# Windowed attention and routed experts: values projected once a token and spread by DMA, turns of normalised tokens a step later

## The chip, the core and the metric

The kernel runs on one core of one Trainium2 chip. TensorE multiplies matrices into PSUM, VectorE and ScalarE read PSUM and SBUF, GpSimd works on SBUF, and SyncE mostly issues DMAs. The metric is the time on the device in microseconds (us) from launch to end. The profile is of one execution; its span goes from the first to the last instruction, and a little of the time lies outside it.

## The reference, cut to what matters

```python
Q = (x @ Wq.T).reshape(B, S, HKV, G, HEAD_DIM)     # B, S = 2, 2048; 4 groups of 4 heads, 8 wide
K = (x @ Wk.T).reshape(B, S, HKV, HEAD_DIM)
V = (x @ Wv.T).reshape(B, S, HKV, HEAD_DIM)
# scores of each token against the 257 tokens around it, softmax, weighted sum of V_win
out = jnp.einsum('bskgw,bswkd->bskgd', attn, V_win).reshape(B, S, HQ * HEAD_DIM) @ Wo.T
x = _layernorm(x + out)
# router: softmax of x @ Wr over 8 experts, the best two, their weights
# expert: (silu(x @ gate) * (x @ up)) @ down, 128 -> 256 -> 128; weighted sum of two
x = _layernorm(x + experts)
```

All of it is float32, and the width of a token is 128.

## The kernel before

The 4096 tokens are 32 tiles of 128 (16 tiles for each of the two sequences) and 8 groups of 512. The attention runs as a loop of steps `s`, written out for each engine by a function `step(s)`; the order of the instructions is fixed by hand, and semaphores carry the dependencies. In step `s` the engines work on several tiles at once:

- TensorE makes the scores of tile `s+2` with queries as rows (`scores_a`, "A items", L736 to L751), from which VectorE takes the largest score (`largest_score`, L1368, L1372, and `negated`, L1381). `maxima(s+1)` (L817) turns the negated maxima of tile `s+1`, ScalarE copies them to `stage` (L1103), and four small DMAs of SyncE (L511) write them as extra rows of `q`.
- TensorE makes the scores of tile `s` again with keys as rows (`scores_b`, "B items", L766 to L787), the maxima included, and ScalarE takes their exponentials (L1095). The three pairs of PSUM banks `pX` go round between A and B items.
- `values(s, 0)` and `values(s-1, n)` (L811) multiply the exponentials by the values `vx`; `sums`, `output` and VectorE finish tile `s-1` (L824, L830, L1416 to L1441).
- Every fourth step (`ln_group`, steps 5, 9, 13, ...) GpSimd runs `norm(m)` for four finished tiles: twelve tiny operations on 128x4 and four of 128x128 (L646), the last of which let the tile be used (`x1_done`).
- `turn(t)` (L835) transposes the normalised tile `t` into `pM`, in the same bank and with the same semaphore step as `maxima(s+1)`; ScalarE copies both out. `x_tile(s)` says which tile: `s - 6`. Four turned tiles are multiplied by the router's weights in `logits` (L840, steps 10, 14, ...).
- The projections of group `n` stand in single steps (`projected(s)`): queries at `4n-7`, keys at `4n-5`, values at `4n-4`; for group 1 at steps -4, -3 and -1. They use one PSUM bank, `pM`, in the order of the dictionary `SMALL`, whose numbers are what the semaphores `m_psum` and `m_evac` count.

The values stand out. `vx` needs a key of 64 tokens on 128 partitions, each half of 32 tokens twice (once for each of two heads of a pair), with a mask of blocks. Before, the host gave `xT` with each 32 tokens written twice, so a group of `xt` has 1024 columns, and `values_of` (L862) makes eight matmuls of 128 of these columns by `wv_sb` (32 wide):

```python
            def values_of(bank, n):
                for c in range(8):
                    mm = pe.matmul(bank[:, c * 32:(c + 1) * 32], xt[:, n % 2, c * P:(c + 1) * P], wv_sb[:],
```

ScalarE copies the 256 columns to `vs`, and GpSimd's `spread_values(n)` (L593) multiplies them by the mask into `vx`, in the step of the projection. In float32 a matmul is two records of the trace.

After the attention the experts run as 44 halves in units `k`, two blocks of 128 rows each (L975 to L1016); the last steps of the attention's tail (`s` from 32, turns and logits among them) are put into the first units by `MOE_STEPS`.

SyncE's queue is in order too: in step `s` first the four rows of maxima, then the writes (`queries_out`) or reads (`queries_in`) of the queries' scratch in HBM, the next `xt`, and other loads.

Of the kernel before, what the change touches and what calls it, by code (L numbers as in the profile page):

```python
# [115 lines left out]
FIRST = -4  # L116
# [68 lines left out]
def x_tile(s):  # L185

    t = s - 6
    return t if 0 <= t < NT else None
# [36 lines left out]
def projected(s):  # L225

    for n in range(1, NGR):
        first = FIRST if n == 1 else 4 * n - 7
        for what, at in (("q", first), ("k", first + (1 if n == 1 else 2)), ("v", first + 3)):
            if s == at:  # L230
                return n, what
    return None
# [26 lines left out]
def attention_moe(nc, x, xT, wq, wk, wv, wo, wr, wgu, wd, consts, out, q_scr, xs, ys):  # L259
    with ExitStack() as ctx:  # L260
# [16 lines left out]
        xt = sb("xt", [P, 2, 2 * GT])  # L277
        vs = sb("vs", [P, 8, 32])
# [79 lines left out]
        v_done = sem("v_done")  # L358
        q_out = sem("q_out")
# [103 lines left out]
        def _(sp):  # L463
            xg = xT.rearrange("d (n t) -> d n t", t=2 * GT)
            sp.dma_start(xt[:, 0, :], xg[:, 0, :]).then_inc(xt_in, 16)
# [5 lines left out]
            sp.dma_start(xt[:, 1, :], xg[:, 1, :]).then_inc(xt_in, 16)  # L471
# [9 lines left out]
            def queries_in(n):  # L481
                sp.wait_ge(q_out, 128 * (n + 1))
                if n >= 2:
                    sp.wait_ge(b_psum, b_done(4 * (n - 2) + 3))
                for j in range(3):
                    read_queries(sp, n, j)

# [16 lines left out]
            def step(s):  # L504
# [9 lines left out]
                for n in range(1, NGR):  # L514
                    if s == (FIRST + 1 if n == 1 else 4 * n - 6):
                        queries_out(n)
                    if s == 4 * n - 4:
                        queries_in(n)
                    if s == 4 * n - 4 and n + 1 < NGR:
                        sp.wait_ge(m_evac, SMALL["v", n])  # L520
                        sp.wait_ge(xt_in, 16 * (n + 1))
                        sp.dma_start(xt[:, (n + 1) % 2, :], xg[:, n + 1, :]).then_inc(xt_in, 16)
# [20 lines left out]
            read_first_queries(sp, 2, 1, 4, q_in)  # L543
            for s in range(FIRST, NT):
                step(s)
# [31 lines left out]
        def _(pool):  # L577
# [10 lines left out]
            def spread_values(n):  # L588
                if n >= 4:
                    t = min(4 * (n - 4) + 4, TPS - 1)  # L590
                    pool.wait_ge(pv_done, ROUND_AT[t, len(rounds(t)) - 1])
# [6 lines left out]
            def project(n, what):  # L598
# [20 lines left out]
                if what == "v":  # L619
                    pool.wait_ge(m_evac, SMALL["v", n])  # L620
                    spread_values(n)
# [4 lines left out]
            pool.wait_ge(v0_copied, 1)  # L626
            pool.wait_ge(s_zero, 2)
            spread_values(0)
# [51 lines left out]
            def step(s):  # L680
                if projected(s) is not None:
                    project(*projected(s))
# [27 lines left out]
        def _(pe):  # L710
# [146 lines left out]
            def tokens(n):  # L857
                return xt[:, n % 2, :].rearrange("p (c o k) -> p c o k", o=2, k=32)[:, :, 0, :]

            def values_of(bank, n):  # L860
                for c in range(8):
                    mm = pe.matmul(bank[:, c * 32:(c + 1) * 32], xt[:, n % 2, c * P:(c + 1) * P], wv_sb[:],  # L862
                                   start=c == 0, stop=True, skip_group_check=True)
# [177 lines left out]
        def _(act):  # L1041
# [10 lines left out]
            act.activation(vs[:].rearrange("p c e -> p (c e)"), pX[1][:, 0, 0:256], ACT.Copy).then_inc(v0_copied, 1)  # L1052
# [15 lines left out]
            def project(n, what):  # L1068
# [7 lines left out]
                else:  # L1076
                    act.wait_ge(v_done, n)
                    act.activation(vs[:].rearrange("p c e -> p (c e)"), pM[:, 0:256], ACT.Copy).then_inc(m_evac, 1)
# [124 lines left out]
        def _(dve):  # L1203
# [253 lines left out]
            dve.tensor_copy(ks[:], pM[:]).then_inc(m_evac, 1)  # L1457

# [155 lines left out]
```

## Time and profile before

| what | value |
|---|---|
| median of 3 runs | 549.03 us |
| lowest and highest of them | 544.09 and 549.33 us |
| time of the profiled execution | 550.67 us |
| its span | 548.8 us |
| TensorE busy in it | 483.2 us (88%) |
| VectorE, ScalarE, GpSimd busy | 363.0, 294.6, 241.8 us |
| mean granted TensorE clock | 0.895 |

The profiled execution is 1.6 us above the median, and 1.9 us of it lie outside the span. The granted clock is a share of 2.4 GHz; it has two levels in this trace, 1.0 and 0.5 (1.2 GHz). The attention ends at about 375 us of the span, the experts' matmuls at about 517 us.

### The profile page before, as it was taken

To read this page: it belongs to the slowest core of one execution; us is meant where nothing else is said; L and a number is where in the kernel's file an instruction comes from. 1 tells how busy PE (TensorE), PEld (TensorE's weight loads), DVE (VectorE), ACT (ScalarE), POOL (GpSimd) and SP (SyncE) were. 2 spreads that over 40 slices of the span, in tenths; PEclk is the share of its full clock that TensorE was granted. 3 is DMA by queue.
4 is the path that set the end of the run, shared out by engine and by line. 5 is a ranking of instruction groups with operands and counts; after the bars stand their busy time and mean duration, and the time that the engine had idled before them with its cause. 6 is when DMAs were issued, how large, how long until landed. Compare 5 with 4: busy or idle time off the path is not lost.

```text
span 548.8 us, 11862 instructions
## 1 busy us (share of the span) xinstructions
PE 483.2 (88%) x3865; PEld 292.4 (53%) x3865; DVE 363.0 (66%) x823; ACT 294.6 (54%) x512; POOL 241.8 (44%) x329
## 2 busy tenths in 40 slices
PE   5699999999998999999999999987999999999700
PEld 2354454454453545344544554434788888888600
DVE  1556867867865446667767888755347765767785
ACT  2125655656655433446556666664565555655551
POOL 2501155455334030223284487600870727776772
PEclk9558999999999555779999999989999999999955
DMA  6633333342235215212621513102242555553462
GB/s 169 99 51 67 80 59 98 79 71 86 42 54 140 39 40 88 68 30 51 127 38 24 98 36 93 41 28 62 76 130 81 164 156 144 146 136 96 107 167 59
DMA packets 84156, 46.92 MB, mean 85 GB/s; under 512 B 40608, under 2 KB 79520, under 8 KB 83424
## 3 DMA queue, kind: packets, MB, share of 16 engines
q1 hardware_dynamic: 65360, 31.04, 25.7%
q0 software_dynamic: 4096, 8.40, 5.7%
q10 hardware_dynamic: 14640, 6.73, 4.4%
q8 instruction: 33, 0.54, 0.5%
q14 instruction: 27, 0.22, 0.1%
HBM read 26.47 MB, written 19.40 MB: 84 GB/s over the span
## 4 chain that ended last, share of the span: by engine, by line
PE 72%; DVE 8%; ACT 6%; POOL 5%; issue 5%; DMA 3%; ACTq 0%; SPq 0%; POOLq 0%; DVEq 0%
PE pV L811 15%; PE pX L736 6%; PE pX L775 6%; PE pX L1016 6%; ACT probs L1095 4%; PE pV L824 4%; PE pX L996 3%; PE pX L998 3%; PE pX L997 3%; PE pX L748 3%; PE pM L862 3%; PE pV L1007 3%; PE pX L787 2%; PE pM L830 2%; PE pX L766 2%
## 5 line engine op out<-in xcount | busy, mean ns | idle before, releaser
L1095 ACT ACTIVATE probs<-pX 128x1024 f32<-128x1024 f32 x152 | 152.9, 1024 | 73.4 <-PE pX L766 58.4
L1368 DVE TENSOR_REDUCE mp<-pX 128x4 f32<-128x1024 f32 (+4 forms) x128 | 150.7, 1185 | 41.0 <-PE pX L740 31.2
L811 PE MATMUL pV<-probs,vx 128*32 128x512 f32 (+1 forms) x736 | 96.1, 589 | 2.4 <-DVE attT L1419 2.0
L676 POOL DMA_INDIRECT probs<-ys,source x64 | 64.5, 1008 | 30.6 <-issue 25.7
L664 POOL DMA_INDIRECT xs<-xr,slot x64 | 63.0, 985 | 31.4 <-issue 17.6
L736 PE MATMUL pX<-kx,q 48*128 48x512 f32 (+4 forms) x256 | 63.3, 494 | 4.2 <-DMA q<-q_scr 4.0
L775 PE MATMUL pX<-q,kx 50*128 50x512 f32 x248 | 64.9, 520 | 0.5 <-DVE mp L1368 0.4
L1471 DVE TENSOR_TENSOR probs<-probs,pX 128x512 f32<-128x512 f32 x44 | 30.2, 686 | 34.4 <-ACT probs L1157 34.4
L1016 PE MATMUL pX<-we,probs 128*128 x352 | 47.0, 276 | 1.1 <-ACT vx L1169 1.1
L1016 PEld LDWEIGHTS pX<-we,probs 128*128 128x128 f32 x352 | 42.7, 192 | 2.0 <-issue 1.9
L1416 DVE RECIPROCAL rden<-pV 128x128 f32<-128x128 f32 x32 | 30.4, 951 | 18.8 <-PE pV L824 18.8
L1157 ACT ACTIVATE probs<-pX 128x512 f32<-128x512 f32 x44 | 26.3, 597 | 30.2 <-PE pX L998 29.2
L775 PEld LDWEIGHTS pX<-q,kx 50*128 50x128 f32 x248 | 25.9, 205 | 26.5 <-issue 17.1
L603 POOL CAST kh<-ks 128x512 fp32r<-128x512 f32 x7 | 4.3, 610 | 78.0 <-ACT ks L1072 78.0
L996 PE MATMUL pX<-we,qh 128*128 x88 | 38.6, 438 | 0.0
L1434 DVE TENSOR_TENSOR xr<-pM,xr 128x128 f32<-128x128 f32 x32 | 9.3, 292 | 39.4 <-PE pM L830 38.9
L736 PEld LDWEIGHTS pX<-kx,q 48*128 48x128 f32 x256 | 27.0, 209 | 14.7 <-POOL kt L605 5.6
L616 POOL CAST qh<-qs 128x512 fp32r<-128x512 f32 x7 | 4.3, 609 | 69.1 <-ACT qs L1075 68.5
L998 PE MATMUL pX<-we,ql 128*128 x88 | 34.7, 394 | 0.0
L997 PE MATMUL pX<-we,qh 128*128 x88 | 34.5, 392 | 0.0
L766 PE MATMUL pX<-mask 64*128 64x256 bf16 (+1 forms) x184 | 31.5, 338 | 0.0
L748 PE MATMUL pX<-kx,q 48*128 48x64 f32 x240 | 21.5, 303 | 9.0 <-ACT probs L1095 8.8
(151 smaller groups left out, 829.1 us busy)
## 6 DMA issues: line engine op xcount, KB each, us to landing
xt<-xs SPq DMA_DIRECT2D x88, 64.0 KB, 1.9
ys<-vx ACTq DMA_DIRECT2D x44, 128.0 KB, 2.1
q<-q_scr SPq DMA_DIRECT2D x42, 128.0 KB
xt<-xT SPq DMA_DIRECT2D x8, 512.0 KB, 5.7
q_scr<-qh SPq DMA_DIRECT2D x32, 64.0 KB, 2.3
q<-stage SPq DMA_DIRECT2D x128, 2.0 KB
xr<-x SPq DMA_DIRECT2D x8, 256.0 KB, 6.0
raw<-wgu SPq DMA_DIRECT2D x4, 512.0 KB, 5.9
```

Of the source, the lines that this page charges most:

```text
L664: pool.indirect_dma_start(xs[ph][:, :], bass.IndirectOffsetOnAxis(ap=slot[:, t, k:k + 1], axis=0), tile(t), None, bounds_check=ROWS - 1, o ...
L676: pool.indirect_dma_start(yin[:, t % YIN, k, :], None, ys[ph][:, :], bass.IndirectOffsetOnAxis(ap=source[:, t, k:k + 1], axis=0), bounds_c ...
L736: mm = pe.matmul(bank[:, pr, 0:64 * (k1 - k0)], q_cols(t, KA, pr, i, i + 1), k_cols(KA, pr, k0, k1), start=True, stop=True, skip_group_che ...
L766: return pe.matmul(bank[:, pr, a * P:b * P].rearrange("p (c g t) -> p c g t", g=G, t=32), mask_rows(pr, M_ONEK, M_ONEK + P), mask_rows(pr, ...
L775: mm = pe.matmul(bank[:, pr, :], k_cols(KB, pr, k0, k0 + 2), q_cols(t, KB, pr, 0, 4), start=True, stop=True, skip_group_check=True)
L811: mm = pe.matmul(pV[row:row + 32, cols], vx[:, chunk, pr, :], src[:, pr, cols], start=n == 0, stop=True, skip_group_check=True)
L996: pe.matmul(to, xh[:, k % 2, rows], hi, start=True, stop=False, skip_group_check=True)
L997: pe.matmul(to, xh[:, k % 2, rows], lo, start=False, stop=False, skip_group_check=True)
L998: mm = pe.matmul(to, xl[:, k % 2, rows], hi, start=False, stop=True, skip_group_check=True)
L1016: mm = pe.matmul(pX[2][:, 1, h * D:(h + 1) * D], hidT[:, k % 2, at:at + P], we[:].bitcast(F32)[:, bass.ds(expert[k, h] + 4 * F + f * D, D) ...
L1095: act.activation(dst, src[:], ACT.Exp).then_inc(exp_done, 1)
L1368: dve.tensor_reduce(mp[:, t % 2, 0, :, i, :], src[:, :, 0:2 * n].rearrange("p r (c v k) -> p r v c k", v=NV, k=32), AX.XY, ALU.max).then_i ...
```

## The change

Turns: `x_tile(s)` becomes `s - 7`, so each `turn(t)` comes one step later. `logits` stays in its step, which now is that of the group's last turn.

Values: `xT` holds each token once, `xt` uses 512 columns a group, and `values_of` makes four matmuls. Their 128 columns go to a new tile `vd` (token on partition), from there by one DMA to a scratch `v_scr` in HBM, and by four DMAs back into `vs` with each 32 tokens on two groups of 32 partitions. SyncE issues both: the write in the step of the projection (`values_out`), the reads a step later (`values_in`). GpSimd's spread comes two steps after the projection. The first two groups are special: group 1's values are projected at step -3, evicted by VectorE, and both groups' reads and spreads stand at steps -2 and -1.

```diff
-FIRST = -4
+FIRST = -5
...
-    t = s - 6
+    t = s - 7
...
-        for what, at in (("q", first), ("k", first + (1 if n == 1 else 2)), ("v", first + 3)):
+        for what, at in (("q", first), ("k", first + (1 if n == 1 else 2)), ("v", first + (2 if n == 1 else 3))):
...
-            sp.dma_start(xt[:, 0, :], xg[:, 0, :]).then_inc(xt_in, 16)
+            xg = xT.rearrange("d (n t) -> d n t", t=GT)
+            sp.dma_start(xt[:, 0, 0:GT], xg[:, 0, :]).then_inc(xt_in, 16)
...
+            def values_out(n):
+
+                wait(sp, v_in[n % 2], 64 * (n // 2))
+                sp.dma_start(v_scr[n % 2].rearrange("(c p) e -> p c e", p=P), vd[:, n % 2]).then_inc(v_out[n % 2], 16)
+
+            def values_in(n):
+
+                sp.wait_ge(v_out[n % 2], 16 * (n // 2 + 1))
+                wait(sp, v_done, n)
+                for a in range(2):
+                    for o in range(2):
+                        row = 64 * a + 32 * o
+                        sp.dma_start(vs[row:row + 32, :, :], v_scr[n % 2].rearrange("(c a k) e -> a k c e", a=2, k=32)[a]
+                                     ).then_inc(v_in[n % 2], 16)
...
+                for n in range(NGR):
+                    if s == (n - 2 if n < 2 else STEP_OF["v", n] + 1):
+                        values_in(n)
+                    if n and s == STEP_OF["v", n]:
+                        sp.wait_ge(m_evac, SMALL["v", n])
+                        values_out(n)
...
             def spread_values(n):
+                pool.wait_ge(v_in[n % 2], 64 * (n // 2 + 1))
...
-                if what == "v":
-                    pool.wait_ge(m_evac, SMALL["v", n])
-                    spread_values(n)
...
             def step(s):
+                for n in range(NGR):
+                    if s == (n - 2 if n < 2 else STEP_OF["v", n] + 2):
+                        spread_values(n)
...
-                return xt[:, n % 2, :].rearrange("p (c o k) -> p c o k", o=2, k=32)[:, :, 0, :]
+                return xt[:, n % 2, 0:GT]
...
-                for c in range(8):
+                for c in range(4):
...
-                    act.wait_ge(v_done, n)
-                    act.activation(vs[:].rearrange("p c e -> p (c e)"), pM[:, 0:256], ACT.Copy).then_inc(m_evac, 1)
+                    wait(act, v_out[n % 2], 16 * (n // 2))
+                    act.activation(vd[:, n % 2].rearrange("p c e -> p (c e)"), pM[:, 0:P], ACT.Copy).then_inc(m_evac, 1)
...
+            dve.wait_ge(m_psum, SMALL["v", 1])
+            dve.tensor_copy(vd[:, 1].rearrange("p c e -> p (c e)"), pM[:, 0:P]).then_inc(m_evac, 1)
```

Three places show how the rows move. First TensorE in step 6, the first with a turn before the change; `nmz` are the negated maxima, `xr` the normalised tile, and the names in brackets are the semaphores waited for. Before:

```order
L811 MATMUL pV<-probs,vx 32x512 [waits exp_done]
L811 MATMUL pV<-probs,vx 32x512 x3
L817 MATMUL pM<-identr,nmz 128x128 [waits nm_done,m_evac,z_done]
L835 MATMUL pM<-cst,xr 128x128 [waits x1_done]
L736 MATMUL pX<-kx,q 128x512 [waits exp_done]
```

and after, at the same place:

```order
L836 MATMUL pV<-probs,vx 32x512 [waits exp_done]
L836 MATMUL pV<-probs,vx 32x512 x3
L842 MATMUL pM<-identr,nmz 128x128 [waits nm_done,m_evac,z_done]
L761 MATMUL pX<-kx,q 128x512 [waits exp_done]
L761 MATMUL pX<-kx,q 128x512
```

The wait for `x1_done` has left this step; the same turn now stands behind the maxima of the next one.

Second TensorE's start, from the values of group 0 to the first A item; the bank `pM` holds the projections of group 1. Before:

```order
L862 MATMUL pX<-wv_sb,xt 128x32 x7
L871 MATMUL pM<-xt,wq_sb 128x512 [waits xt_in]
L869 MATMUL pM<-xt,wk_sb 128x512 [waits xt_in,m_evac]
L736 MATMUL pX<-kx,q 128x256 [waits s_const,q_first,v0_copied,k_ops,q_split]
...
L740 MATMUL pX<-mask 128x64 x2
L862 MATMUL pM<-wv_sb,xt 128x32 [waits xt_in,m_evac]
L862 MATMUL pM<-wv_sb,xt 128x32 x7
L736 MATMUL pX<-kx,q 128x512 [waits a_max]
```

and after:

```order
L887 MATMUL pX<-wv_sb,xt 128x32 x3
L896 MATMUL pM<-xt,wq_sb 128x512 [waits xt_in]
L894 MATMUL pM<-xt,wk_sb 128x512 [waits xt_in,m_evac]
L887 MATMUL pM<-wv_sb,xt 128x32 [waits xt_in,m_evac]
L887 MATMUL pM<-wv_sb,xt 128x32 x3
L761 MATMUL pX<-kx,q 128x256 [waits s_const,q_first,v0_copied,k_ops,q_split]
```

Group 1's values moved from between two A items to the place ahead of the first, and are four matmuls and not eight.

Third SyncE's queue at the start, from the first reads of queries to the rows of maxima of tile 0 (`q<-stage`). Before:

```order
L447 DMA q<-q_scr 16x1536 x4
L433 DMA q_scr<-qh 512x1x32 [waits q_split]
L433 DMA q_scr<-qh 512x1x32 x3
L433 DMA q_scr<-ql 512x1x32 [waits q_split]
L433 DMA q_scr<-ql 512x1x32 x3
L511 DMA q<-stage 1x4x128 [waits m_evac]
```

and after:

```order
L450 DMA q<-q_scr 16x1536 x4
L494 DMA v_scr<-vd 128x4x32 [waits v0_copied]
L436 DMA q_scr<-qh 512x1x32 [waits q_split]
L436 DMA q_scr<-qh 512x1x32 x3
L436 DMA q_scr<-ql 512x1x32 [waits q_split]
L436 DMA q_scr<-ql 512x1x32 x3
L494 DMA v_scr<-vd 128x4x32 [waits m_evac]
L503 DMA vs<-v_scr 32x8x32 [waits v_out0]
L503 DMA vs<-v_scr 32x8x32 x3
L529 DMA q<-stage 1x4x128 [waits m_evac]
L529 DMA q<-stage 1x4x128 x3
L503 DMA vs<-v_scr 32x8x32 [waits v_done,v_out1]
```

Six DMAs now stand between the reads of queries and the maxima of tile 0, and four more behind these.

## Rows read from the trace of the kernel before

**Rows 1.** The page: granted clock in 40 slices, shares of the chain.

```profile
PEclk9558999999999555779999999989999999999955
...
PE 72%; DVE 8%; ACT 6%; POOL 5%; issue 5%; DMA 3%; ACTq 0%; SPq 0%; POOLq 0%; DVEq 0%
```

**Rows 2.** The chain that ended last: start us, us, engine, tile, line, count.

```profile
26.24 3.55 PE pM L862 x16
...
74.79 1.90 PE pM L862 x16
...
210.54 3.55 PE pM L862 x16
```

**Rows 3.** What TensorE waited for: us in total, times, longest.

```profile
PE pX L748 <- ACT probs L1095: 8.8, 22, 0.5
...
PE pM L835 <- POOL xr L646: 3.0, 4, 1.9
...
PE pM L849 <- issue: 0.7, 1, 0.7
```

**Rows 4.** The timeline around 175 us, ScalarE and TensorE; idle before in brackets.

```profile
170.04 0.60 ACT L1075 ACTIVATE qs<-pM 128x512 f32<-128x512 f32 x1 [0.86 <-PE pM L871]
...
176.98 0.30 PE L835 MATMUL pM<-cst,xr 128*128 128x128 f32 x1 [1.90 <-POOL xr L646]
```

**Rows 5.** Windows: length, busy PE, PEld, DVE, ACT, POOL, then clock, DMA share, GB/s.

```profile
177.00:178.00 1.00, 1.00 (x7) 0.47 (x11) 0.24 (x1) 0.41 (x2) 1.00 (x2) 0.69 0.06 16
...
178.00:224.00 46.00, 45.92 (x259) 22.94 (x252) 23.80 (x48) 15.95 (x24) 6.88 (x8) 0.50 0.30 58
225.00:232.00 7.00, 5.86 (x65) 3.29 (x67) 5.24 (x8) 4.70 (x9) 2.63 (x6) 0.99 0.26 77
...
225.00:226.00 1.00, 1.00 (x10) 0.73 (x10) 0.22 (x2) 0.43 (x3) 0.00 (x0) 0.92 0.00 0
...
232.00:239.00 7.00, 7.00 (x34) 2.51 (x26) 4.11 (x16) 2.05 (x2) 4.73 (x12) 0.51 0.01 2
...
371.00:379.00 8.00, 5.98 (x59) 3.18 (x52) 3.54 (x13) 2.05 (x6) 0.00 (x0) 1.00 0.25 68
```

**Rows 6.** The chain: values and an A item at either clock.

```profile
143.17 0.43 PE pX L736 x2
...
151.28 1.00 PE pV L811 x8
...
185.74 1.86 PE pV L811 x8
...
189.50 0.72 PE pX L736
```

**Rows 7.** VectorE's timeline around the first values among A items.

```profile
30.64 1.23 DVE L1368 TENSOR_REDUCE mp<-pX 128x4 f32<-128x1024 f32 x1 [2.67 <-PE pX L740]
```

**Rows 8.** The start: a piece of the chain, and a window.

```profile
1.19 4.68 DMA wq_sb<-wq
...
4.00:8.00 4.00, 1.99 (x3) 0.99 (x4) 0.00 (x0) 0.00 (x0) 0.00 (x0) 1.00 0.95 287
```

**Rows 9.** SyncE's and TensorE's timeline at the start, and the scratch's DMAs.

```profile
21.25 2.64 SPq L433 DMA_DIRECT2D q_scr<-ql  x4
25.10 10.93 SPq L511 DMA_DIRECT2D q<-stage  x8
...
33.90 0.77 PE L775 MATMUL pX<-q,kx 50*128 50x512 f32 x2
...
L511 SPq DMA_DIRECT2D q<-stage x12: 572/573/727, 25.1 to 46.8; - x12
...
DMA to landing us min/median/max: 1.9/2.3/3.4
```

**Rows 10.** TensorE's timeline in a unit with turns and logits.

```profile
390.02 1.06 PE L840 MATMUL pM<-wr_sb,x1T 128*128 128x8 f32 x8 [0.35 <-ACT x1T L1107]
391.40 0.30 PE L835 MATMUL pM<-cst,xr 128*128 128x128 f32 x1 [0.32 <-issue]
```

More of the change, by code:

```diff
@@ L256, in k_ready, with attention_moe @@
     return 5 * n + 4
-def attention_moe(nc, x, xT, wq, wk, wv, wo, wr, wgu, wd, consts, out, q_scr, xs, ys):
+def attention_moe(nc, x, xT, wq, wk, wv, wo, wr, wgu, wd, consts, out, q_scr, v_scr, xs, ys):
     with ExitStack() as ctx:
@@ L277, in attention_moe @@
         xt = sb("xt", [P, 2, 2 * GT])
+        vd = sb("vd", [P, 2, 4, 32])
         vs = sb("vs", [P, 8, 32])
@@ L358, in attention_moe @@
         v_done = sem("v_done")
+        v_out = [sem(f"v_out{i}") for i in range(2)]
+        v_in = [sem(f"v_in{i}") for i in range(2)]
         q_out = sem("q_out")
@@ L463, in _ @@
         def _(sp):
-            xg = xT.rearrange("d (n t) -> d n t", t=2 * GT)
-            sp.dma_start(xt[:, 0, :], xg[:, 0, :]).then_inc(xt_in, 16)
+            xg = xT.rearrange("d (n t) -> d n t", t=GT)
+            sp.dma_start(xt[:, 0, 0:GT], xg[:, 0, :]).then_inc(xt_in, 16)
             sp.dma_start(wq_sb[:], wq).then_inc(s_wq, 16)
@@ L470, in _ @@
             sp.wait_ge(xt_in, 16)
-            sp.dma_start(xt[:, 1, :], xg[:, 1, :]).then_inc(xt_in, 16)
+            sp.dma_start(xt[:, 1, 0:GT], xg[:, 1, :]).then_inc(xt_in, 16)
             def queries_out(n):
@@ L521, in step @@
                         sp.wait_ge(xt_in, 16 * (n + 1))
-                        sp.dma_start(xt[:, (n + 1) % 2, :], xg[:, n + 1, :]).then_inc(xt_in, 16)
+                        sp.dma_start(xt[:, (n + 1) % 2, 0:GT], xg[:, n + 1, :]).then_inc(xt_in, 16)
+                for n in range(NGR):
[4 more added lines that the diff above has]
+                        values_out(n)
                 if s % 4 == 0 and 0 <= s < NT:
@@ L543, in _ @@
             read_first_queries(sp, 2, 1, 4, q_in)
+            sp.wait_ge(v0_copied, 1)
+            values_out(0)
             for s in range(FIRST, NT):
@@ L625, in _ @@
             spread_keys(0, 1).then_inc(k_ops, 1)
-            pool.wait_ge(v0_copied, 1)
             pool.wait_ge(s_zero, 2)
-            spread_values(0)
             def norm(m):
@@ L1051, in _ @@
             act.wait_ge(p0_psum, 3)
-            act.activation(vs[:].rearrange("p c e -> p (c e)"), pX[1][:, 0, 0:256], ACT.Copy).then_inc(v0_copied, 1)
+            act.activation(vd[:, 0].rearrange("p c e -> p (c e)"), pX[1][:, 0, 0:P], ACT.Copy).then_inc(v0_copied, 1)
             act.wait_ge(k_ops, 2)
@@ L1590 @@
         "x": x,
-        "xT": np.ascontiguousarray(np.broadcast_to(
-            x.T.reshape(D, TOK // 32, 1, 32), (D, TOK // 32, 2, 32)).reshape(D, 2 * TOK)),
+        "xT": np.ascontiguousarray(x.T),
         "wq": np.ascontiguousarray(
@@ L1608 @@
     q_scr = nc.dram_tensor("q_scr", (2, 2, NR, 16, GT // 32, G, 32), F32, kind="Internal").ap()
+    v_scr = nc.dram_tensor("v_scr", (2, GT, KV * HD), F32, kind="Internal").ap()
     xs = [nc.dram_tensor(f"xs{b}", (ROWS, D), F32, kind="Internal").ap() for b in range(NPH)]
     ys = [nc.dram_tensor(f"ys{b}", (BLOCKS[b] * P, D), F32, kind="Internal").ap() for b in range(NPH)]
-    attention_moe(nc, *ins, out, q_scr, xs, ys)
+    attention_moe(nc, *ins, out, q_scr, v_scr, xs, ys)
     r = run_bass_kernel_spmd(nc, [arrays], core_ids=[0])
```

## The prediction

> **What bounds the kernel now.** I read the page first, then the chain of waits, then what TensorE waited for, and last the windows around each change of its clock. The page and the chain say one thing: TensorE is the bound. It has 72% of the chain, and what other engines have of it is mostly short hand-overs inside a step [rows 1]. So what takes time off TensorE in the attention counts almost in full, and what moves on other engines counts only if TensorE comes to wait for it. Three sorts of time on TensorE's path bear on this change.
>
> The value projections stand in the chain with their whole length: sixteen records, 1.90 us where the clock is full and 3.55 us where it is half [rows 2]. Five groups have the first price, and group 5 (at 210.54) and group 1 (at 26.24) the second.
>
> The turns wait for GpSimd four times, 3.0 us in all, 1.9 of it once [rows 3]. The code and the timeline show why: in steps 5, 9, 13 and 21 ScalarE takes the queries of a group from PSUM (at 170.04), GpSimd splits them, and only then starts `norm`; the turn of the next step stands behind that. The long one is at the seam of the two sequences, where TensorE's step is short, so that it comes to the turn early [rows 4].
>
> The clock is the third and largest. In the page's row of slices it is at half speed from about 177 us to 225 [rows 1], and the window 178 to 224 has TensorE busy for 45.92 of 46.00 us at 0.50 [rows 5]. The last thing that TensorE did before the clock fell was to sit idle for those 1.90 us, until 176.98 [rows 4]; half a microsecond later every matmul takes the longer time. It fell once more at 232, after a stretch of 7 us with 1.1 us idle, and was back at 239 [rows 5].
>
> **The change part by part.** The sum is against the profiled execution, 550.67 us.
>
> (a) Values of groups 2 to 7: four matmuls for eight, so half of the records. Half of 5 x 1.90 + 3.55 is 6.5 us. Nothing else takes their place: what follows in those steps (the sums of the tile before) waits for a copy that ScalarE has finished by then, since in steps with no values at this place TensorE goes on without a stop. Gain 6.5; if a third of it turned into a wait for that copy, 4.4, which I take as the lower bound.
>
> (b) Values of group 1 leave the A items and go to the idle time before them. There TensorE did nothing for 4 us while the first queries went to HBM and back, and eight records at the slow clock are 1.8 us; VectorE's extra copy of 128 columns falls in the same gap. Of the 3.55 us freed only VectorE's idle time is won, as the maxima become the bound: 2.67 us before its reduction at 30.64 [rows 7]. Gain 2.6, bounds 2 and 3.5.
>
> (c) The turns' waits for GpSimd, 3.0 us, go [rows 3]. A turn a step later has some 10 us more, and the tile was late by 0.4 to 1.9 us. Next in line is the wait for ScalarE's exponentials at L748, which each step has anyway.
>
> (d) The first load of `xt` is 256 KB for 512 KB, and the weights of the queries queue behind it: at 287 GB/s 256 KB take 0.9 us [rows 8]. TensorE's first matmul waited for that weight. Gain 0.9, bounds 0 and 1.8.
>
> (e) One turn more lies in the experts' part: that of tile 31 goes to the unit with the last logits, which then waits for ScalarE's copy of it. The nearest rows show 0.35 us for such a wait and 0.32 us ahead of a turn [rows 10]. Loss 0.7, bounds 0.3 and 1.5.
>
> (f) SyncE has 40 DMAs more. In the running loop they stand behind the rows of maxima of their step, and whatever they wait for (a write a step old, a spread three steps old) is long there; the next rows come about 7 us later, against 4 x 0.6 us of issuing. GpSimd's spread waits for reads issued a step before, the keys of the next group are queued behind it, and TensorE asks for these values another step later. All that is free. At the start it isn't: SyncE issues until 23.9 without a pause and takes the rows of maxima of tile 0 at 25.10 [rows 9]. Two writes (0.63 us each) and four reads (taken as 0.57 us each, the price of a small one [rows 9]) come to 3.5 us, of which 1.2 us was free: the rows go out about 2.3 us later, the last at 29.9, and land, with the 1.9 us of the quickest scratch DMA, at 31.8. TensorE's first B item needs them; it was at 33.90 and by (b) would be at 31.3. That is 0.5 us; with a hand-over more I take a loss of 0.7, bounds 0 and 2, since no row of before has four such reads ahead of the maxima.
>
> These pieces are of 128 bytes. The row of the scratch's DMAs, whose pieces are of 128 bytes too, shows 2.3 us to landing [rows 9], as quick as others. The Trainium skill (DMA: Bandwidth & Descriptors, Specifications) says that transfers run at line rate only from 512 bytes, and that smaller ones are read, modified and written. By that rule term (f) would be at its upper end; by the row it is at 0.7.
>
> (g) The clock. The stretch at half speed is 47.8 us long: the shares 0.69 and 0.92 of two windows of 1 us put its ends at 177.4 and 225.2 [rows 5]. The same eight records take 1.86 us in it and 1.00 outside, an A item 0.72 and 0.43 [rows 6]; with a ratio of 1.75, between the two, its work would take 27.3 us, 20.5 less, or 0.43 us for each slow one. Off this go 1.5 us for three waits at L748 of 0.45 us that a full clock brings back, and 0.8 us that (a) counts already at the slow price. Gain 18.2 if the stretch doesn't come, 0 if it does. I take that it doesn't, because the one long idle time in the attention lies directly ahead of it and is the very wait that (c) removes, and because with it gone TensorE has work without a stop on both sides of that place. Against it speaks that the clock fell at 232 after much less idle time, and that it did not fall between 371 and 379, with 2 us idle of 8 [rows 5]: idle time alone doesn't decide.
>
> Sum without (g): 6.5 + 2.6 + 3.0 + 0.9 - 0.7 - 0.7 = 11.6, so 539.1 us. With (g): 29.8, so **521 us**, against a median of 549.03. The profiled execution is 1.6 us over that median, probably by the length of the slow stretch; as the forecast has no such stretch, I leave it.
>
> **The rivals.** First, the stretch stays whole: the work at the seam of the sequences is light (short A items), and the clock falls there for that, not for the idle time. Then 539 us, and the profile has one row of slices with four or five low digits near the middle, as now. For it speaks the fall at 232; against it that at the start of the first sequence, with the same light items, the clock rose.
>
> Second, the stretch at the seam goes, but one of another length opens later, at the wait of the ranks (L849, 0.7 us [rows 3]), which the change leaves. Before, that cost 6.8 us at half speed, which the forecast still holds. If it lasts 27 us, 20 more x 0.43 = 8.6 us, so 530 us. The rows have nothing that sets an end: TensorE was busy throughout for 46 us and the clock stayed down [rows 5]. The Trainium skill (TensorE: Matmul & The Clock Gate, What's actually happening) says that activity releases the throttle. By that rule a stretch with a busy TensorE is short, and the time would be 521; the row speaks against it.
>
> Third, even the short stretches go or shrink: the 6.8 us one gives 2.9 us, and the one of the start (it rose at 44.3, at half speed from 13.5) up to 5. Then 513 us.
>
> Fourth, slower than before: the slow stretch of the start grows. The change takes TensorE's work out of step -1 and puts a wait for SyncE's late rows into step 0, so TensorE is less busy while the clock is low. If it stayed low for 47.8 us more, as it could at 178, and the seam's stretch stayed too, the cost is 20.5 us: 560 us. It decides from 23 us of added slow time (9.9 / 0.43). Against it: all of it must come together.
>
> That the change misses its aim, in that TensorE waits for the turns again a step later, I give nothing: at the worst place the tile came 1.9 us after the turn asked for it, and a step is 8 us or more.
>
> **How the numbers follow.** The lower bounds of the gains with the upper ones of the losses make a to f 5.9 us, the other ends 14.5. So the forecast 521 stands for 518 to 527: 0.58. Second stretch, 527 to 536: 0.17. Whole stretch, 536 to 545, with 0.03 of it above 543.5: 0.18. Third, 510 to 515: 0.05. Slower: 0.02. The range 515 to 541 leaves out the last two and the tail of the whole stretch, about 0.12. A measurement of this kernel can tell 1% from no change; faster by more than that (below 543.5) is 0.95, within it 0.03, slower 0.02.
>
> **What would show it.** (a) In the page L862's successor has half the records, and chain pieces of 0.95 us. (c) The wait of turns for GpSimd is gone from TensorE's list. (g) The row of slices has no run of fives in the middle, and the mean clock is about 0.935 for 0.895 (half of 47.8 us less lost, over 519). (b, f) The maxima of tile 1 come 2.6 us earlier against those of tile 0, and the first B item waits for a DMA for up to 1 us. (d) The first matmul starts about 0.9 us earlier. (e) A wait for ScalarE's copy before the last logits. The forecast is wrong if the clock falls near the seam with no idle time ahead of it, or if the start stays slow past 45 us.

## The result, and the profile after

The changed kernel takes 523.83 us, the median of 4 runs (522.45 to 529.63). The kernel before, run beside it, takes 546.56 us, the median of 4 runs (541.52 to 549.33). The ratio is 0.961, with a 95% interval of 0.950 to 0.973: faster, by 15 to 27 us. (The ratios, and the medians called near-fastest further down, leave out executions over 1.5% above the fastest of their kernel; all other medians hold every run.) The profiled execution took 522.57 us, its span is 520.6.

The two rows of the page that answer to [rows 1], of the kernel after:

```profile
PEclk9999999999999999999999699969999999999955
...
PE 69%; DVE 12%; ACT 6%; issue 5%; DMA 2%; SPq 2%; POOL 2%; POOLq 0%; ACTq 0%; DVEq 0%
```

The run of fives in the middle is gone. Two single digits lower than 9 stand later, at 291 and at 339 us. GpSimd's share of the chain fell from 5% to 2% and VectorE's rose from 8% to 12%: TensorE waits for the turns no longer, and VectorE's maxima are more often on the path.

The chain, with values at full clock and the load of `xt` for group 2 (start us, us, engine, tile, line, count); compare [rows 2]:

```profile
36.41 5.91 DMA xt<-xT
...
70.94 1.01 PE pM L887 x8
...
110.18 1.01 PE pM L887 x8
...
150.63 1.01 PE pM L887 x8
```

Eight records of 1.01 us in all stand where sixteen of 1.90 stood. What TensorE waited for (us in total, times, longest); compare [rows 3]:

```profile
PE pX L773 <- ACT probs L1120: 8.7, 22, 0.5
PE pX L975 <- DMA wq_sb<-wq: 5.4, 1, 5.4
PE pX L800 <- DVE mp L1393: 2.1, 7, 0.4
...
PE pV L836 <- DVE attT L1444: 1.9, 3, 1.0
...
PE pM L865 <- ACT x1T L1132: 0.9, 2, 0.4
...
PE pM L874 <- issue: 0.7, 1, 0.7
...
PE pM L896 <- DMA xt<-xT: 0.7, 1, 0.7
```

The row of the turns behind GpSimd is gone. The waits of B items for VectorE's maxima (L800) grew from two of 0.4 us in all to seven of 2.1. The same row before:

```profile
PE pX L775 <- DVE mp L1368: 0.4, 2, 0.2
```

New are one wait for `xt` (L896) and a second wait for ScalarE's copy ahead of logits (L865).

The windows (length, busy PE, PEld, DVE, ACT, POOL, clock, DMA share, GB/s); the second is the stretch that was at 0.50 in [rows 5]:

```profile
177.00:178.00 1.00, 1.00 (x14) 0.58 (x14) 0.44 (x3) 0.42 (x3) 0.00 (x0) 1.00 0.00 0
178.00:224.00 46.00, 42.91 (x419) 21.32 (x411) 40.48 (x79) 26.81 (x42) 16.09 (x27) 1.00 0.39 81
...
291.00:302.00 11.00, 10.67 (x60) 4.64 (x60) 6.48 (x16) 4.25 (x6) 8.26 (x10) 0.53 0.15 48
...
339.00:349.00 10.00, 8.85 (x45) 3.72 (x38) 3.76 (x14) 1.72 (x4) 0.00 (x0) 0.50 0.23 66
```

In the same 46 us TensorE now has 419 records instead of 259, VectorE 79 instead of 48, and TensorE shows 3 us of idle time that it had not: at full clock the other engines are the bound for moments. Two stretches at 1.2 GHz, of 10 us each, came at 291 and 339.

The start, SyncE's and TensorE's timeline; compare [rows 9]:

```profile
17.80 0.42 SPq L494 DMA_DIRECT2D v_scr<-vd  x1
...
23.68 0.62 SPq L494 DMA_DIRECT2D v_scr<-vd  x1
24.34 2.02 SPq L503 DMA_DIRECT2D vs<-v_scr  x4
26.40 2.62 SPq L529 DMA_DIRECT2D q<-stage  x4
```

```profile
5.38 1.19 PE L975 MATMUL pX<-xt,wq_sb 128*128 128x512 f32 x1 [5.38 <-DMA wq_sb<-wq]
...
31.81 0.80 PE L800 MATMUL pX<-q,kx 50*128 50x512 f32 x2 [0.23 <-DVE mp L1393]
```

The first matmul starts at 5.38 us, not 6.01. The rows of maxima of tile 0 go out at 26.40 us instead of 25.10. No B item at the start waits for a DMA; the only wait there is 0.23 us, for VectorE.

Where the 28.1 us between the two profiled executions lie can be read from the start of the matmul that turns the maxima of each tile (L817 before, L842 after), which comes once a step:

| start of the maxima of tile | before, us | after, us | earlier by, us |
|---|---|---|---|
| 0 | 24.32 | 23.49 | 0.8 |
| 1 | 32.83 | 29.24 | 3.6 |
| 15 | 174.75 | 167.08 | 7.7 |
| 16 | 192.92 | 176.87 | 16.1 |
| 19 | 238.54 | 205.76 | 32.8 |
| 27 | 321.03 | 286.40 | 34.6 |
| 28 | 331.06 | 300.48 | 30.6 |
| 31 | 357.25 | 327.04 | 30.2 |
| end of span | 548.8 | 520.6 | 28.2 |

The seam of the sequences (tiles 15 to 19) holds 25.1 us, the rest of the attention ahead of it 7.7. Some 4 us are given back at 291. Behind the maxima of tile 31 it is 2 us net: 1.5 more are won where the kernel before had one more short stretch at half speed (3.4 us, at 361.7), and the stretch at 339 costs 3.4.

### The profile page after: what moved, and what is told of

It is laid out like the page before. It is cut to its first block, busy times and chain, and to the rows that moved or that the text cites. A ratio compares the mean times of both kernels' runs of the same rounds, so it can differ in the third digit from the quotient of the medians.

```text
span 520.6 us, 11785 instructions
## 1 busy us (share of the span) xinstructions
PE 459.7 (88%) x3801; PEld 277.9 (53%) x3801; DVE 364.2 (70%) x824; ACT 293.3 (56%) x511; POOL 241.5 (46%) x329
## 4 chain that ended last, share of the span: by engine, by line
PE 69%; DVE 12%; ACT 6%; issue 5%; DMA 2%; SPq 2%; POOL 2%; POOLq 0%; ACTq 0%; DVEq 0%
PE pV L836 14%; PE pX L1041 6%; PE pX L761 5%; PE pX L800 5%; ACT probs L1120 4%; PE pX L1021 4%; PE pX L1023 3%; PE pX L1022 3%; DVE mp L1393 3%; PE pV L849 3%; PE pX L773 3%; PE pV L1032 3%; PE pM L855 3%; PE pX L812 3%; PE pX L791 2%
## 5 line engine op out<-in xcount | busy, mean ns | idle before, releaser
L836 PE MATMUL pV<-probs,vx 128*32 128x512 f32 (+1 forms) x736 | 90.2, 558 | 2.1 <-DVE attT L1444 1.9
L698 POOL DMA_INDIRECT probs<-ys,source x64 | 64.0, 1000 | 30.6 <-issue 25.5
L800 PE MATMUL pX<-q,kx 50*128 50x512 f32 x248 | 62.4, 500 | 2.1 <-DVE mp L1393 2.1
L761 PE MATMUL pX<-kx,q 48*128 48x512 f32 (+4 forms) x256 | 60.5, 473 | 0.8 <-POOL kt L632 0.5
L1498 DVE TENSOR_TENSOR probs<-probs,pX 128x512 f32<-128x512 f32 x44 | 30.2, 687 | 34.8 <-ACT probs L1182 34.8
L800 PEld LDWEIGHTS pX<-q,kx 50*128 50x128 f32 x248 | 24.7, 195 | 26.6 <-issue 13.3
L761 PEld LDWEIGHTS pX<-kx,q 48*128 48x128 f32 x256 | 25.7, 199 | 9.9 <-DVE mp L1393 1.1
L791 PE MATMUL pX<-mask 64*128 64x256 bf16 (+1 forms) x184 | 30.3, 325 | 0.0
L1136 ACT COPY po<-pV 128x512 f32<-128x512 f32 x32 | 18.7, 585 | 18.4 <-PE pV L836 18.4
```

The costliest lines, as they stand in the source:

```text
L698: pool.indirect_dma_start(yin[:, t % YIN, k, :], None, ys[ph][:, :], bass.IndirectOffsetOnAxis(ap=source[:, t, k:k + 1], axis=0), bounds_c ...
L761: mm = pe.matmul(bank[:, pr, 0:64 * (k1 - k0)], q_cols(t, KA, pr, i, i + 1), k_cols(KA, pr, k0, k1), start=True, stop=True, skip_group_che ...
L791: return pe.matmul(bank[:, pr, a * P:b * P].rearrange("p (c g t) -> p c g t", g=G, t=32), mask_rows(pr, M_ONEK, M_ONEK + P), mask_rows(pr, ...
L800: mm = pe.matmul(bank[:, pr, :], k_cols(KB, pr, k0, k0 + 2), q_cols(t, KB, pr, 0, 4), start=True, stop=True, skip_group_check=True)
L836: mm = pe.matmul(pV[row:row + 32, cols], vx[:, chunk, pr, :], src[:, pr, cols], start=n == 0, stop=True, skip_group_check=True)
```

## The experiments

Four questions: is it the idle time at the seam that brings the long stretch at half speed; are the turns or the values what the change lives on; does the later turn matter by itself; what opens the stretches that remain. Twelve experiments ran (nine kernels, three of them twice), in three jobs, each job on one chip with the kernel before beside it. The spread of one kernel's runs is wide, and for the kernel before the near-fastest median is far below that of all runs, so the table has both. In the third job a disturbance that I can't name added over 100 us to every kernel, so its times stand against each other alone.

| job | kernel | median us (runs) | near-fastest median us (runs) | lowest, highest | stretches at half speed from 50 to 480 us in the profiled execution |
|---|---|---|---|---|---|
| 1 | before | 548.06 (13) | 537.13 (6) | 535.32, 565.57 | no trace |
| 1 | values alone | 553.58 (4) | 549.12 (2) | 546.01, 559.38 | 173-190, 204-211, 218-221, 310-334, 364-378 |
| 1 | turns alone | 529.57 (4) | 524.67 (2) | 524.23, 564.43 | 178-181 |
| 1 | before, norm first | 529.80 (4) | 524.61 (2) | 521.46, 547.38 | 342-359 |
| 1 | change, idle put back at the seam | 544.75 (10) | 538.47 (5) | 537.24, 562.71 | 134-137, 171-223 |
| 2 | before | 551.65 (11) | 531.29 (1) | 531.29, 579.29 | no trace |
| 2 | change | 525.03 (6) | 524.65 (5) | 522.51, 539.84 | 193-207, 210-213 |
| 2 | change, idle elsewhere | 531.88 (4) | 531.28 (3) | 530.63, 541.89 | 134-145, 199-220 |
| 2 | change, `xt` early | 534.63 (4) | 529.45 (2) | 527.52, 537.95 | 171-215, 219-222, 355-369 |
| 2 | change, `xt` early, ranks late | 530.86 (4) | 520.85 (1) | 520.85, 532.98 | 193-207, 299-323 |
| 3 | before | 677.22 (23) | 666.80 (6) | 662.51, 700.34 | no trace |
| 3 | change, old turns, norm first | 659.17 (6) | 658.84 (4) | 657.05, 679.99 | 193-197, later ones |
| 3 | values alone | 674.40 (12) | 660.60 (2) | 658.84, 697.37 | 171-181, 209-212, later ones |
| 3 | turns alone | 675.83 (6) | 654.46 (1) | 654.46, 690.26 | 142-145, 183-187, later ones |
| 3 | change | 666.93 (12) | 648.95 (1) | 648.95, 678.90 | 134-137, 192-206, 209-212, later ones |

### The values alone

The changed kernel with the turns in their old step:

```diff
-    t = s - 7
+    t = s - 6
```

> The change with the turns left where they were (one step earlier); the values are spread as in the change. Theory (the idle time at the seam lets the clock fall): the wait of 1.9 us is back in the step at the seam and with it a stretch at half speed of 40 us or more, so 536 to 543 us and a mean clock near 0.90. Rival (the light work at the seam, thinned by fewer value matmuls or not, decides): no such stretch, only the waits of some 2 us come back, 524 to 528 us.

Measured: 553.58 us against 548.06 (ratio 1.032, 1.021 to 1.043, from two of its runs and six of before), and in the third job, where it was run again, 674.40 against 677.22 (ratio 0.999, 0.985 to 1.013). The values alone bought nothing; in the first job they were even slower, above the range expected, and why is open. The wait is back, and the clock falls right behind it, at 173.2, though for 17 us and not for the 40 expected; the timeline of the execution of job 1 around the seam and the window behind it:

```profile
173.19 0.45 PE L860 MATMUL pM<-cst,xr 128*128 128x128 f32 x1 [1.90 <-POOL xr L668]
```

```profile
174.00:190.00 16.00, 15.92 (x90) 7.81 (x88) 7.14 (x13) 5.97 (x8) 2.08 (x3) 0.50 0.22 34
```

The direct gain is there (tile 15 at 170.96 us against 174.75, although the clock of the start rose 3 us later), and is lost again in stretches of 65 us together, against 58 before. The rival, that the values do without the turns what the two do together, falls.

### The turns alone

The kernel before with one number changed:

```diff
-    t = s - 6
+    t = s - 7
```

> The kernel before with the turns a step later and nothing else. Theory: no idle time at the seam, no long stretch at half speed, 524 to 532 us. Rival (the saving is in the values and the start): 543 to 547 us, with the long stretch still there.

Measured: 529.57 us against 548.06, by the near-fastest medians 524.7 against 537.1. That is nearly the whole gain, with the values as they were. Its row of slices in the page:

```profile
PEclk9659999999999899999999999999999999999955
```

The step across the seam (tile 15 to 16) takes 11.3 us, of which a stretch of 3.4 us is at half speed; it took 18.2 before.

### Norm first, turns where they were

The same wait is removed another way: GpSimd does a group's norm ahead of its split of queries.

```diff
             def step(s):
+                if s < 28 and ln_group(s) is not None:
+                    norm(ln_group(s))
                 if projected(s) is not None:
...
-                if ln_group(s) is not None:
+                if s >= 28 and ln_group(s) is not None:
                     norm(ln_group(s))
```

> The kernel before with GpSimd's order changed in steps 5 to 25: norm of a group ahead of the split of the next queries or keys, the turns in their old step. The tile is then ready before the turn asks. Theory (the wait, not the place of the turn): as turns only, 524 to 532 us, no wait of TensorE for GpSimd at a turn. Rival (the turn in that step, with its bank and its copy, matters by itself): 540 us or more.

Measured: 529.80 us (near-fastest 524.6), the same as with the later turns, and the seam's step takes 9.8 us. So it isn't the later turn as such that the change lives on, but that TensorE doesn't stand idle there.

### The idle time put back

The changed kernel, in which the turn of tile 7 waits for one tile more, which GpSimd finishes later:

```diff
-                pe.wait_ge(x1_done, t + 1)
+                pe.wait_ge(x1_done, t + 2 if t == 7 else t + 1)
```

> The change with one thing more: the turn of tile 7 (step 14, at the seam) also waits for tile 8 to be normalised, as the turn there did before. Nothing else moves. Theory: an idle time of 1.9 us at about 167 us, the clock falls behind it and stays down for tens of us, 538 to 546 us. Rival (idle time is not what lets the clock fall): only the idle time itself, 524 to 527 us.

Measured: 544.75 us, ratio to before 1.005 (0.997 to 1.012). One wait of 1.9 us takes back the whole gain. The change itself did not run in this job; beside the turns alone, which did, this kernel is 15 us slower (14 by the near-fastest medians). The timeline at the seam and the window behind it, of this kernel:

```profile
170.55 0.30 PE L860 MATMUL pM<-cst,xr 128*128 128x128 f32 x1 [1.90 <-POOL xr L668]
```

```profile
172.00:222.00 50.00, 49.92 (x274) 23.68 (x274) 27.92 (x57) 18.04 (x28) 6.40 (x7) 0.50 0.29 52
```

This is the picture of [rows 4, 5] again: 1.90 us idle, then 50 us with TensorE busy at 0.50.

### The same idle time in a full step

```diff
+                pe.wait_ge(x1_done, t + 4 if t == 3 else t + 1)
```

> The change with one thing more: the turn of step 10, in the middle of the first sequence, also waits for the third tile of the norm before it, some 2 us. As long an idle time as at the seam, in a full step. If idle time alone lets the clock fall: the clock falls at about 130 us and stays down for tens of us, 538 to 546 us. If it takes idle time and the light work of the seam together: only the 2 us, 525 to 530 us, with no slow stretch behind 130 us.

Measured: 531.88 us, 6.9 above the change in the same job, between the two times expected. The wait is at 132.79 us, in the middle of the first sequence; the timeline and the window of this kernel:

```profile
132.79 0.30 PE L860 MATMUL pM<-cst,xr 128*128 128x128 f32 x1 [1.95 <-POOL xr L668]
```

```profile
135.00:144.00 9.00, 9.00 (x61) 5.23 (x59) 4.50 (x6) 2.94 (x4) 2.54 (x2) 0.50 0.39 61
```

The clock fell behind it here too, but was back after 10 us (134 to 145). The step took 16.1 us for 10.0: 1.9 of idle time and 4.2 of half clock. So idle time lets the clock fall anywhere; at the seam, where the steps are light, the stretches behind the same wait were 10, 17, 48 and 51 us long (values alone twice, before, idle put back). One execution in a full step is few against four, but in the first two jobs, from 50 us on, stretches over 24 us were seen at the seam alone.

### The change as the measure of job 2

The change unaltered.

> The change itself, unaltered, beside the other kernels of this job: 522 to 530 us, 3 to 5% faster than before.

Measured: 525.03 us against 551.65. Its profiled execution has a stretch of 13.7 us at half speed that the first one had not. What stands directly ahead of it, in the timeline of TensorE, and its window:

```profile
191.60 0.50 PE L800 MATMUL pX<-q,kx 50*128 50x512 f32 x2 [0.28 <-DVE mp L1393]
192.73 0.59 PE L800 MATMUL pX<-q,kx 50*128 50x512 f32 x2 [0.35 <-DVE mp L1393]
```

```profile
193.00:206.00 13.00, 13.00 (x74) 5.73 (x72) 9.34 (x21) 4.73 (x8) 0.00 (x0) 0.50 0.57 90
```

The pair of waits for VectorE belongs to the row of L800 that grew with the change. In the execution above the same pair stood at 189.04 and 190.17, and the clock stayed up.

### `xt` of group 2 early, and the ranks later

The first kernel loads `xt` of group 2 a step earlier; the second also puts the ranks of step 17 behind two more items, on TensorE and on ScalarE.

```diff
-                    if s == 4 * n - 4 and n + 1 < NGR:
+                    if s == (-1 if n == 1 else 4 * n - 4) and n + 1 < NGR:
```

```diff
-                if s in RANK_AT:
+                if s in RANK_AT and s != 17:
...
                 a_item(s + 2, 3)
+                if s == 17:
+                    wait(pe, z_done, min(s - 1, NT))
+                    pe.wait_ge(m_evac, SMALL["rk", RANK_AT[s]] - 1)
+                    ranks(RANK_AT[s])
                 b_item(s, 3)
```

> The change with the load of group 2's tokens issued one step earlier, ahead of the reads of queries and of the second reads of values. If SyncE's longer queue at the start made this load late: TensorE's wait of 0.7 us for it before the queries of group 2 is gone, and the maxima of tile 2 come 0.7 us earlier, 522 to 526 us. If the DMA engines are what is late: the wait stays.

> As the one before, and the ranks of step 17 stand behind two more score items on TensorE, their copy behind one more exponential on ScalarE: TensorE's wait of 0.7 us for them goes. 520 to 525 us; if such waits are what opens the remaining slow stretches, the lowest runs come under 518 us, and if not, it is as the one before.

Measured: 534.63 and 530.86 us, neither better than the change (525.03), and both above what was expected; no run came under 518 us. Both small waits went, so the load was late by SyncE's queue, but the times follow the clock. The profiled execution of the first has 44 us at half speed at the seam with no wait for a turn ahead of it; its timeline:

```profile
170.98 0.85 PE L773 MATMUL pX<-kx,q 48*128 48x64 f32 x6 [0.54 <-ACT probs L1120]
```

So 0.54 us can be enough there, a wait that the change has as well (0.5 is the longest of L773 above) and that left the clock alone in its own execution. Whether the early load has a part in it these few runs don't tell.

### All on one chip: old turns with norm first, and three again

The changed kernel with its turns in the old step and GpSimd's norm ahead of the spread of values and the split of queries (the edits of the two sections above together):

```diff
-    t = s - 7
+    t = s - 6
...
             def step(s):
+                if s < 28 and ln_group(s) is not None:
+                    norm(ln_group(s))
                 for n in range(NGR):
```

> The changed kernel with its turns back in the old step (tile s-6), and GpSimd's norm of a group ahead of its spread of values and its split of queries in steps below 28: the turns' wait for GpSimd is gone by another order, the values are projected once. What matters by my theory is that TensorE has no idle time at the seam, however that is got: 521 to 527 us, within 1% of the change in the same job, no wait of turns for GpSimd over 0.5 us, and no stretch at half speed over 15 us at 165 to 225 us. Rival: the later turn itself (other work beside it) is what the change lives on: then 535 us or more, with the stretch of the seam back.

> The same kernel as the experiment with the values alone (changed kernel, turns of tile s-6), beside the others on one chip: the wait for GpSimd at the seam stays. If its slowness in the first job was how the slow stretches fell there, it comes out within 2% of the kernel before (540 to 555 us). If the new values cost time when the turns wait (GpSimd's spread ahead of norm makes the tile later), it is again 2% or more slower than the kernel before in the same job.

> The kernel before with the turns a step later, nothing else, beside the change on one chip. The values' direct gain is 9.1 us by the forecast (6.5 in groups 2 to 7, 2.6 at the start) and was 0.9 us a step by the traces. If slow stretches don't depend on it, this kernel is 7 to 10 us slower than the change. The first job gave 529.6 against 524 of another job, 5 us; rival: half of the values' gain is given back in clock, 3 to 6 us.

> The change unaltered, as the measure for the three others of this job: 522 to 528 us.

None of the times came near what was expected: from some 250 us on, the four kernels whose traces I have lose time to waits of several us, up to 22, which the profile puts down to nothing in the kernel. A piece of the chain of the change in this job:

```profile
320.35 8.47 another core or an unknown queue
...
330.12 5.05 another core or an unknown queue
```

The times thus tell little: the new order has a ratio of 0.986 to before (0.977 to 0.995), and 659 us against 667 for the change, with lists that overlap (the change has the lowest run, 648.95). The traces up to 180 us are undisturbed (the milestones agree with those of the first two jobs), and there they answer the first question once more. From tile 15 to 16 the kernels take 9.79 us (norm first), 9.79 (change), 11.30 (turns alone), and 15.85 (values alone, the only one with the 1.90 us wait). The window of 165 to 190 us of the kernel with norm first:

```profile
165.00:190.00 25.00, 24.36 (x223) 11.73 (x222) 18.59 (x38) 16.05 (x26) 10.86 (x13) 1.00 0.38 92
```

The turn is in its old step here and the clock stays up. The rival (that the change lives on the later turn) falls by this; by its time alone, it would have stayed open. How much the values add to the turns is open: 524 and 525 us against 529.6 by the medians of different jobs, 524.65 against 524.67 by the near-fastest ones, and no direct comparison that is undisturbed.

### What stands ahead of each fall

With all these traces at hand I looked, for each fall of the clock between 50 and 370 us, at TensorE's last wait of 0.3 us or more ahead of it. The profiled executions of before, of the change and of the first two jobs have 23 falls, and every one has such a wait, of 0.34 to 1.95 us, that ended at most 1.8 us before it (or within 0.2 us of it, the precision of this reading). It is the turn's wait for GpSimd four times (1.9 us; stretches of 10, 17, 48 and 51 us), the pair of waits for VectorE's maxima (L800) in step 17, or a single one near 300 us, seven times (0.34 to 0.36; 7 to 24 us), ScalarE's exponentials nine times (0.39 to 0.54; 3 to 14 us, once 44), and VectorE's transposed attention three times (0.6 and 1.0; 3 to 17 us). Four of the nine come right behind the ranks' wait of 0.73 us, and are short (3 to 7 us). The kernel that has the ranks later has none at that place.

The seven falls behind L800 tell what became of the values' gain. All seven are in kernels with the new values. In the first two jobs those kernels wait 1.1 us or more there between 40 and 380 us. The three with the old values (before, turns alone, norm first) wait 0.2 us, and show no fall behind such a wait. With fewer matmuls of values TensorE comes to the B items before VectorE is done, and part of what it saves goes into that wait and the clock behind it. How large that part is no run measures.

That is more than chance: in the change's trace 30 waits of 0.34 us or more stand between 40 and 370 us, and the 1.8 us behind each make up 54 us of these 330, so that a fall at a random moment would find one in 16 of 100 cases. The reverse doesn't hold: of these 30 waits only two were followed by a fall. The wait ahead of the fall at 339, in TensorE's timeline of the change:

```profile
338.76 0.92 PE L836 MATMUL pV<-probs,vx 128*32 128x512 f32 x4 [0.97 <-DVE attT L1444]
```

## Why the prediction was right

The forecast was 521 us, the median is 523.83, and the mechanism is the one that carried it. Point by point:

- **(a) Values of groups 2 to 7**, 6.5 us forecast. At full clock eight records take 1.01 us for 1.90: 0.89 us a group, five times, and group 5, which the stretch held, half of 3.55: 6.2 in all. No wait for ScalarE's copy took their place, but that nothing else would was wrong: the waits for VectorE's maxima at L800 grew by 1.7 us. From tile 17 to 18, where the values of group 5 stand, the change takes 9.96 us and the turns alone, at full clock too, 10.36: a gain of 0.4, not 0.9.
- **(b) Group 1**, 2.6 forecast. From tile 0 to tile 1 the maxima take 5.75 us instead of 8.51: 2.76.
- **(c) The turns' waits**, 3.0 forecast. They are gone. The three small ones were worth a little more than their idle time: the kernel before takes 9.62 us from tile 7 to 8, 10.54 from 11 to 12 and 10.53 from 23 to 24, the change 8.95, 10.01 and 10.01. With these 0.67, 0.53 and 0.52 and the 1.9 of the seam, 3.6.
- **(d) The first load**, 0.9 forecast, 0.63 measured at the first matmul.
- **(e) The last turn**, 0.7 loss forecast. L865 waits twice, 0.9 us, where it waited once, 0.4: a loss of 0.5. The two units that hold it take 10.75 us for 9.83, so with the turn itself it is 0.9.
- **(f) SyncE's 40 DMAs**, 0.7 loss forecast, at the first B item. The size holds and the place was wrong. The reads of the scratch go out at 0.5 us each and the rows of maxima at 26.40, 1.3 us late and not 2.3; the B item didn't wait. But ten more DMAs, 4.9 us of issuing, stand ahead of the load of `xt` for group 2. It went out at 36.41, 2.5 us earlier than before (38.92), while TensorE came to the query projection that needs it 4.5 us earlier (41.75 for 46.27) and waited 0.7 us. I had looked for who needs the rows, and not for the last in the queue. In the second job's execution, where the clock rose at 46 us, this wait didn't show. The reads landed after a median of 1.9 us, the writes to `v_scr` only after 5.5, where the writes of the queries' scratch, of pieces as small, took 2.2; TensorE waited for neither. So the row of before was the better guide for the time. The Trainium skill (DMA: Bandwidth & Descriptors, Specifications) has transfers below 512 bytes off the line rate; the trace doesn't contradict it, but no time here changes by it.
- **(g) The clock**, 18.2 forecast. (Its three waits of 0.45 us make 1.35 and not 1.5, which changes nothing.) In the pair of executions compared it came, whole: with 1.9 for the wait itself, 1.8 for values at the slow price and some 2.9 for the stretch at 232 that went too, 24.8 is what one would add up for tiles 15 to 19, and they show 25.1. The experiment that puts 1.9 us of idle time back at the seam loses the gain, and two different ways of taking the wait away win it: 18 us by the medians of all runs, 12 by the near-fastest ones.

Right for its mechanism, but that the size fits so well is in part luck. Term (g) prices the stretch as there (48 us) or not there, and it is neither: the kernel before doesn't show it each time. Two of its executions in job 1, at 536.65 and 537.95 us, had mean clocks of 0.951 and 0.957, where the change had 0.953; a stretch of 48 us takes 0.044 off the mean (half of 47.8 over 548.8) and the end of the span, at 0.54 for 29 us, another 0.024, so they can't hold one unless the record leaves out more than a start. And one small edit to the change (`xt` early) had 44 us at half speed at the seam with no wait for a turn. The execution from which the forecast reckoned had the long stretch, and the four runs of before beside the change (541.52 to 549.33 us) lie above most of the faster ones of job 1. By the near-fastest medians the gain is 12 us for the turns alone in job 1, and 7 for the change in job 2, where the kernel before has a single such run.

The time came out a little above the forecast, which held that one 6.8 us stretch would stay as it was and no other would come; it also missed the 3.4 us stretch that the kernel before had at 361.7. Instead of it came two of 10 us, at 291 and 339, that cost 4 and 3 us; in the next execution one of 13.7 at 193. That is the second rival, partly and with another cause than it named: it spoke of the ranks' wait (0.73 us, which now stands at 199.16 with the clock at 1.00 on both sides), and what precedes the stretches is VectorE's and ScalarE's lag, which a TensorE at full clock runs into. The third rival was right for the start in this execution: A items there take 746 ns at half and 457 at full clock, and the change came at 38.6 us for 44.3, though the granted clock of the first windows prints 1.00; so the mean of 0.953 that the page gives leaves out the start's stretch (with it I estimate 0.92, from 33 us at half speed of 520.6), and the 0.935 of the forecast is met by the next execution's 0.929.

```profile
L761 PE MATMUL pX<-kx,q 48*128 48x512 f32 x18 | 6.5, 746 | 0.0
```

(Groups by form, 18 to 38 us, of the kernel after; the same group from 40 to 70 us has 457 ns.)

The prediction named as a sign against itself that the clock falls near the seam with no idle time ahead. It did fall there again in several executions, but with 0.34 us or more ahead each time. So the ground given for (g), that TensorE has work without a stop there once the turn's wait is gone, doesn't quite hold. The other sign, a start that stays slow past 45 us, was a poor one: in the second job the change's start lasted until 46.2, with a time of 524.65 us. What the runs show: idle time of 1.9 us at the seam lets the clock fall: in all four profiled executions that have it a stretch of 10 to 51 us followed, and removing it alone wins 18 us by the medians of all runs, 12 by the near-fastest ones. What stays open: why one of the many shorter waits lets the clock fall and the others don't, and what ends a stretch. The spread of the kernel before (531 to 579 us on one chip) is most likely the same thing, as the mean clocks above suggest, but no trace was taken of it. Taking VectorE's lag out of the light steps, which these waits point to, was not tried. The page of the Trainium skill on this (TensorE: Matmul & The Clock Gate, What's actually happening) says that activity releases the throttle; windows of 50 us at 0.50 with TensorE busy for 49.92 speak against that as an account of the length.

## What to carry to other kernels

Where the granted clock falls, read TensorE's last wait ahead of the fall first: one wait of 1.9 us cost here some six to ten times its length, and the cheapest remedy was to change the order on the engine that was late (one number or two lines), while halving a whole class of matmuls won nothing that could be measured as long as the wait stood. Price an idle time at a light place of the program by what the clock may do behind it, and look next for the waits that the faster engine will run into. When matmuls are taken out of a step, look which engine TensorE then waits for in it. And of DMAs added to a queue, follow the whole queue to its last user, since the one that waits may stand further down than the next.

## What the runs showed of the hardware that was not expected

- The same idle time has no fixed price: 10 us at half speed behind 1.95 us in a full step, 10 to 51 us behind 1.90 in a light one, with TensorE busy throughout either stretch (9.00 of 9.00 us, 49.92 of 50.00).
- All 23 falls of the first two jobs' executions and of the pair first compared came at most 1.8 us behind a wait of TensorE (or within 0.2 us of its end), some of 0.34 us only; most such waits pass without one, and the same kernel falls behind one in one execution and behind another in the next.
- The granted clock can print 1.00 at the start of a trace while matmuls take the longer time (746 ns for 457).
- On the chip of the third job, or at that hour, the same kernels took some 120 to 150 us longer, with waits of up to 22 us that nothing in the kernel explains.
